# First mixture's results added to the residual inside the masked readout

## The chip, the cores and the metric

One core of one Trainium2 chip runs the whole program. The metric is device time in microseconds (us) of one execution. The kernel before took 2452.74 us, the median of 3 runs (2448.83 to 2454.53).

## The reference, cut to what matters

The reference is four layers, each an attention and a feed-forward part on x of 16 x 128 tokens x 256 numbers (B = 16 tiles of P = 128 rows, D = 256), float32. The change lies between the feed-forward part of layer 0 (a mixture of 8 experts, each token sent to 2) and the attention of layer 1 (a readout of a memory under a mask):

```python
x = x + _L0_ffn_ref(...)      # ends in: return hidden + moe_out, moe_out = the sum of two experts' weighted rows
x = x + _L1_xattn_ref(_layernorm(x), ctx_2048, mask)
x = x + _L1_ffn_ref(_layernorm(x), ...)           # ternary weights, inputs rounded to 8 bits

def _L1_xattn_ref(hidden_states, memory_tokens, memory_mask):
    scores = jnp.einsum('bsd,bmd->bsm', hidden_states, memory_tokens) * scale
    scores = jnp.where(memory_mask[:, None, :], scores, neg_inf)
    attn = jax.nn.softmax(scores, axis=-1)
    readout = jnp.einsum('bsm,bmd->bsd', attn, memory_tokens)
    return jnp.where(valid_b[:, None, None], readout, jnp.zeros_like(readout))
```

So the row that layer 1 starts from is (residual + hidden) + first expert's row + second expert's row.

## The kernel before, in words

The program is a chain of stages, each a block with a list of instructions for each of the five engines; an engine goes on to the next block when all engines have ended theirs. A stage works on pairs of tiles (PAIR = 2, so NI = 8 pairs, 128 x 512 numbers each). Waits are on semaphores, and the order of the work on each engine is written out by hand, the loops being unrolled.

`mixture0` (L1370) runs 39 blocks of 128 rows through the experts. TensorE first issues 18 matmuls of no use (`keep_busy`, L175), and then for each block turns the rows, multiplies and turns again. VectorE scales the results, and GpSimd scatters them by indirect DMAs into the DRAM tensor `expert_rows` (`taken`), the first expert's rows in its first half and the second's in its second half. Between the scatters GpSimd adds residual and hidden of each pair into `xk` (`residual_in`, L1498). When the last scatter has landed, `collect` (L1447) loads the two rows of each token back, four pairs in flight, VectorE's `combine` adds them (L1596 first expert's row plus `xk`, L1600 plus the second's), and SyncE stores each pair to `residual1`. The first pair is loaded again into `head` by `hand_on` (L162).

`mask_bit` (L3584) is the next stage. Its loop runs over steps i = 0 to 9; in a step the attention of pair i, the first feed-forward half of pair i-1 and the second of pair i-2 stand side by side. VectorE's list for a step is `softmax(i)`, `quantise2(i-2)` (it ends in the second rounding, two L3898), `product` (L3867), `readout(i)` (L3817 a reciprocal, L3820 a product of 128x2, L3824 the sum with x), `stats(i)`, `product`, `x_stats(i+1)` (L3791 to L3796), `product`, `quantise(i)` (L3843 to L3859), `x_norm(i+1)` (L3803), `product`, `residual(i-2)`, `subln(i-1)`. GpSimd's list is `rstd(i)` (L3698), `gain(i-1, 0)` (L3708), `x_rstd(i+1)` (L3694), `gain(i-1, 1)`, `rstd2(i-1)` (L3702). SyncE loads x (L3663) and the context (L3664, L3665) three pairs ahead into rings of XR = 3, waiting for `x2`, and stores the results. Stages that follow are not touched but for the counts of the two shared semaphores that are handed to them.

Of the kernel before, what the change touches and what calls it, by code (L numbers as in the profile page):

```python
# [1369 lines left out]
def mixture0(nc, k, x_in, src_in, out, spread, taken, arena, spare, bi, load_next, hand, ternary):  # L1370
# [7 lines left out]
    with ExitStack() as ctx:  # L1378
# [3 lines left out]
        def w(name):  # L1382
# [8 lines left out]
            gathered0 gathered1 gathered2 gathered3 first_added y stored0 stored1""")  # L1391
# [5 lines left out]
        xk = sb("xk", [P, B, D])  # L1397
# [7 lines left out]
        yg = spare[:, 0:16 * D].rearrange("p (r c t d) -> p r c t d", r=4, c=2, t=PAIR)  # L1405
        acc = spare[:, 16 * D:20 * D].rearrange("p (r t d) -> p r t d", r=2, t=PAIR)
        y = k["y"][:, hand["side"]].rearrange("p (r j d) -> p r j d", r=2, j=PAIR)
# [17 lines left out]
        @block.sync  # L1425
        def _(sp):
            def load_h(i):
                if i == NI - 1:
                    sp.wait_ge(k["last_stored"], hand["last"])
                if i >= 5:  # L1430
                    sp.wait_ge(s["res"], i - 3)
                sp.dma_start(h_pair(i), pair_of(src_in, i)).then_inc(s[f"h_loaded{i % 4}"], 16)

            def load_x(r, a, b):
                sp.dma_start(xk[:, a:b], x_in[a:b].rearrange("t p d -> p t d")).then_inc(s[f"x_loaded{r}"], 16)

            def load_rows(n, at):
                if n >= RR_:
                    sp.wait_ge(sent[f"kept_stored{n % YR}"], (n - RR_) // YR * 16 + 16)
                sp.dma_start(rows[:, n % RR_], spread[bass.ds(at, P)]).then_inc(s[f"rows_loaded{n % RR_}"], 16)  # L1440

            def collect(i):
                if i >= 4:
                    sp.wait_ge(s["y"], i - 3)
                for c in range(2):
                    first = (c * B + i * PAIR) * P
                    sp.dma_start(yg[:, i % 4, c], taken[first:first + PAIR * P].rearrange("(t p) d -> p t d", p=P)).then_inc(s[f"gathered{i % 4}"], 16)  # L1447

            def store(i):
                sp.wait_ge(s["y"], i + 1)  # L1450
                sp.dma_start(pair_of(out, i), y[:, i % 2]).then_inc(k["last_stored"] if i == NI - 1 else s[f"stored{i % 2}"], 16)

            sp.wait_ge(sent["scattered0"], 18 * 16)
            sp.wait_ge(sent["scattered1"], 14 * 16)
            for n in range(NB):
                load_rows(n, sp.value_load(bi[0:1, 1, n:n + 1], min_val=0, max_val=ROWS_SPREAD - P))
                if n == 3:
                    load_next[0](sp, s["weights_next"])
                if n == 8:
                    load_h(1)  # L1460
                    load_x(0, 2, 4)
                    load_h(2)
                    load_h(3)
                    load_x(1, 4, 8)
                    load_h(4)
                    load_x(2, 8, 16)
                if n in (16, 20, 24):
                    load_h(n // 4 + 1)
            for r in range(YR):
                sp.wait_ge(sent[f"kept_stored{r}"], (NB - r + YR - 1) // YR * 16)  # L1470
            for i in range(4):
                collect(i)
            for i in range(NI):
                store(i)
                if i + 4 < NI:
                    collect(i + 4)
                if i == 1:
                    sp.wait_ge(s["res"], 1)
                    sp.wait_ge(s["stored0"], 16)
                    hand_on(sp, k, hand)  # L1480
            for r in range(2):
                sp.wait_ge(s[f"stored{r}"], (NI // 2 - r) * 16)
            load_next[1](sp, s["weights_next"])
# [78 lines left out]
        def _(dve):  # L1562
# [30 lines left out]
            def combine(i):  # L1593
                dve.wait_ge(s[f"gathered{i % 4}"], (i // 4 + 1) * 32)
                dve.wait_ge(s["res"], i + 1)
                nc.vector.tensor_tensor(flat(acc[:, i % 2]), flat(yg[:, i % 4, 0]), flat(pair(xk, i)), ALU.add).then_inc(s["first_added"], 1)  # L1596
                dve.wait_ge(s["first_added"], i + 1)
                if i >= 2:
                    dve.wait_ge(s[f"stored{i % 2}"], i // 2 * 16)
                nc.vector.tensor_tensor(flat(y[:, i % 2]), flat(yg[:, i % 4, 1]), flat(acc[:, i % 2]), ALU.add).then_inc(s["y"], 1)  # L1600

# [11 lines left out]
            for i in range(NI):  # L1613
                combine(i)

        @block.tensor
        def _(pe):
# [34 lines left out]
            keep_busy(nc, k, 7, 18)  # L1652
# [1931 lines left out]
def mask_bit(nc, k, x_in, x_out, ctx_T, ctx_rows, masks, arena, load_next, hand, ternary):  # L3584
# [7 lines left out]
    with ExitStack() as ctx:  # L3592
# [3 lines left out]
        def w(name):  # L3596
# [4 lines left out]
            x_loaded0 x_loaded1 x_loaded2 t_loaded0 t_loaded1 t_loaded2 c_loaded0 c_loaded1 c_loaded2 stored0 stored1  # L3601
# [13 lines left out]
        xt = sb("xt", [P, XR, PAIR, D])  # L3615
# [25 lines left out]
        def x_pair(i):  # L3641
            return k["head"][:, 0] if i == 0 else xt[:, i % XR]

        def x_ready(eng, i):
            if i == 0:
                eng.wait_ge(k["first_loaded"], hand["first"])
            else:
                eng.wait_ge(s[f"x_loaded{i % XR}"], (i // XR + (i % XR > 0)) * 16)
# [6 lines left out]
        def _(sp):  # L3655
            def load(i):
                if i >= XR:
                    sp.wait_ge(s["x2"], i - XR + 1)
                pair = slice(i * PAIR, (i + 1) * PAIR)
                if i == NI - 1:  # L3660
                    sp.wait_ge(k["last_stored"], hand["last"])
                if i >= 1:
                    sp.dma_start(xt[:, i % XR], pair_of(x_in, i)).then_inc(s[f"x_loaded{i % XR}"], 16)  # L3663
# [25 lines left out]
        def _(pool):  # L3689
            nc.gpsimd.memset(ones[:], 1.0).then_inc(s["constants"], 1)  # L3690

            def x_rstd(i):
# [17 lines left out]
            x_rstd(0)  # L3710
            clear_spent(nc, k)
            for i in range(NI + 1):
# [4 lines left out]
                at(rstd2, i - 1)  # L3717

# [68 lines left out]
        def _(dve):  # L3787
            def x_stats(i):
# [119 lines left out]

            x_stats(0)
# [131 lines left out]
def build(nc, x, ctx_T, out, packs):  # L4041
# [8 lines left out]
    with ExitStack() as ctx:  # L4050
# [59 lines left out]
        with ExitStack() as kept:  # L4110
# [7 lines left out]
            mixture0(nc, k, res[0], hid, res[1], spread[0], taken[0], arena[0], arena[1][:, words(W_BIT):], bi, loader("bit", W_BIT, 1), hand(2, 4, 4, x1), ternary)  # L4118
            mask_bit(nc, k, res[1], res[0], ctx_T, x["ctx"], x["mask"], arena[1], loader("xatt2", W_XATT2, 0), hand(3, 5, 5, x0), ternary)
        xatt2(nc, k, res[0], res[1], ctx_T, arena[0], loader("arrow", W_ARROW, 1), hand(4, 6, 6, x1))  # L4120
        arrow(nc, k, res[1], res[0], arena[1], loader("qkv3", W_QKV3, 0), hand(5, 7, 8, x0))
        with ExitStack() as kept:
# [7 lines left out]
            qkv3(nc, k, res[0], ctx_T, qT, steps, KT, V, v_step, arena[0], nothing, hand(6, 8, 10), q_rows, q_ahead)  # L4130
            attend3(nc, k, qT, steps, att, KT, V, v_step, arena[0], loader("moe3", W_MOE3, 1), hand(7, 10, 12, x0, (1, att)), q_ahead)
        mixture3(nc, k, res[0], att, out, spread[1], taken[1], arena[1], arena[0], hand(8, 12, 14))
# [100 lines left out]
```

## Time and profile before

| what | value |
|---|---|
| median of 3 runs | 2452.74 us |
| the profiled execution, its own time | 2454.85 us |
| span of the profiled execution | 2453.1 us |
| mean granted TensorE clock | 0.944 of full speed |
| busy: TensorE, VectorE, ScalarE, GpSimd | 86%, 74%, 61%, 28% of the span |
| `expert_rows` loaded back | 32 DMAs of 256 KB in two stages, 4.6 us from issue to landing (median) |

The span runs from the first to the last instruction of one execution. Busy shares are averages over stages that have different limits; the rows of the next but one section are of the two stages in question.

### The profile page before, as it was taken

Reading aid. Unit: us, or ns where it says so; the run is one execution under the profiler, and the core shown is the slowest. Engines: PE = TensorE matmul, PEld = TensorE weight load, DVE = VectorE, ACT = ScalarE, POOL = GpSimd, SP = SyncE. Lnnn points to the kernel's source line nnn. Section 1 sums busy time; section 2 is a strip of 40 time slices with the busy share of each in tenths; the row PEclk is TensorE's granted clock in tenths of the full one; section 3 lists DMA queues with packets and bytes.
Section 4 is the critical chain, followed back from the end, with each engine's and each line's share of the span. In section 5 each row is a group of like instructions: output and inputs, shape, how many; then the busy total and the mean of one; then the engine's idle time right before and its main releaser. Section 6 shows DMA issues by size and latency. Waiting matters only on the chain. (4 is left out here: it accounts for less than half of the span.)

```text
span 2453.1 us, 49624 instructions
## 1 busy us (share of the span) xinstructions
PE 2111.5 (86%) x17715; PEld 1432.1 (58%) x17715; DVE 1805.0 (74%) x4336; ACT 1498.7 (61%) x2838; POOL 676.8 (28%) x820
## 2 busy tenths in 40 slices
PE   6987999999869748769979877899999999998897
PEld 4663666666646524447746665555555555556675
DVE  6866778788632358866647779899999999995434
ACT  4553666666524326634434445899999999993332
POOL 2214333535333413332213214211111111113532
PEclk9997999999979869989989999899999999999899
DMA  5543111211135251021010033466655655552234
GB/s 193 161 149 122 54 44 44 70 42 57 40 101 185 62 197 57 14 85 38 25 46 27 20 103 100 151 120 116 118 117 120 124 119 115 119 110 72 79 98 141
DMA packets 380704, 230.05 MB, mean 94 GB/s; under 512 B 270106, under 2 KB 372270, under 8 KB 379440
## 3 DMA queue, kind: packets, MB, share of 16 engines
q1 hardware_dynamic: 373648, 210.03, 32.2%
q0 software_dynamic: 6816, 16.86, 1.9%
q8 instruction: 146, 2.39, 0.4%
q14 instruction: 94, 0.77, 0.1%
HBM read 86.48 MB, written 77.68 MB: 67 GB/s over the span
## 5 line engine op out<-in xcount | busy, mean ns | idle before, releaser
L3488 DVE CUSTOM_DVE_ANT_0 arena<-psum,attend_zero,queries_step 128x1024 f32<-128x1024 f32 x512 | 622.4, 1279 | 13.6 <-PE psum L3537 13.2
L3462 ACT ACTIVATE attend_ex<-arena,attend_mx 128x2048 uint16<-128x2048 f32 x256 | 523.7, 2046 | 6.7 <-POOL attend_mx L3440 3.0
L3537 PE MATMUL psum<-keys_turned,queries_ahead 96*128 96x512 bf16 x1024 | 318.7, 394 | 41.7 <-DVE attend_mx L3488 25.4
L3562 PEld LDWEIGHTS psum<-values,attend_pw 128*128 128x128 f16 x4096 | 178.4, 97 | 124.5 <-issue 8.7
L3440 POOL TENSOR_SCALAR attend_mx<-attend_mx 128x1 f32<-128x1 f32 x256 | 73.9, 289 | 572.0 <-DVE attend_mx L3488 572.0
L3553 PE MATMUL psum<-keys_turned,ident_b 96*128 96x512 bf16 x510 | 195.1, 383 | 0.0
L3562 PE MATMUL psum<-values,attend_pw 128*128 128x16 f16 x4096 | 178.7, 170 | 0.2 <-DVE attend_pw L3509 0.2
L3467 ACT COPY attend_pw<-psum 128x512 f32<-128x512 f32 x263 | 161.4, 617 | 15.0 <-PE psum L3547 14.9
L3547 PE MATMUL psum<-ident_b,attend_ex 128*128 128x128 bf16 x2128 | 166.5, 222 | 3.6 <-ACT attend_pw L3467 1.4
L3547 PEld LDWEIGHTS psum<-ident_b,attend_ex 128*128 128x128 bf16 x2128 | 142.6, 99 | 40.9 <-ACT attend_ex L3462 6.6
L3537 PEld LDWEIGHTS psum<-keys_turned,queries_ahead 96*128 96x128 bf16 x1024 | 71.7, 99 | 120.6 <-DVE attend_mx L3488 109.1
L845 POOL TENSOR_TENSOR gqa_nq<-gqa_nq,neg_half 128x20 f32<-128x20 f32 x16 | 88.3, 5516 | 142.0 <-DVE gqa_nq L1042 142.0
L1255 PE MATMUL psum<-arena,gqa_hT 128*128 128x512 f32 x256 | 113.5, 596 | 0.0
L1343 PE MATMUL psum<-arena,gqa_pT 128*128 128x256 f32 x512 | 113.1, 379 | 0.0
L1343 PEld LDWEIGHTS psum<-arena,gqa_pT 128*128 128x128 f32 x512 | 97.3, 190 | 20.1 <-issue 7.7
L935 ACT ACTIVATE gqa_pr<-gqa_pr,gqa_mx 128x128 f32<-128x128 f32 x256 | 98.9, 390 | 6.5 <-DVE gqa_mx L1064 6.5
L848 POOL TENSOR_TENSOR gqa_ra<-gqa_ra,gqa_nq 128x2560 f32<-128x2560 f32 x16 | 71.5, 4467 | 49.6 <-DVE gqa_ra L1052 49.6
L1255 PEld LDWEIGHTS psum<-arena,gqa_hT 128*128 128x128 f32 x256 | 48.1, 192 | 55.6 <-issue 55.2
L177 PE MATMUL psum<-ident_b 128*128 128x512 bf16 x221 | 60.8, 420 | 10.7 <-PEq L707 8.5
L1064 DVE CUSTOM_DVE_ANT_0 gqa_pr<-psum,gqa_cmask 128x128 f32<-128x128 f32 x256 | 57.6, 287 | 16.6 <-PE psum L1276 12.7
L1276 PE MATMUL psum<-gqa_qkT 128*128 128x128 f32 x512 | 64.3, 280 | 0.0
L2851 POOL TENSOR_TENSOR arrow_outer<-arrow_vr,arrow_nr 128x1024 f32<-128x1024 f32 x16 | 30.9, 1932 | 117.2 <-DVE arrow_vr L2945 117.2
(578 smaller groups left out, 4920.9 us busy)
## 6 DMA issues: line engine op xcount, KB each, us to landing
spread_rows<-zeros SPq DMA_DIRECT2D x34, 1032.0 KB
moe_rows<-spread_rows SPq DMA_DIRECT2D x78, 129.0 KB, 2.1
arena<-expert_rows SPq DMA_DIRECT2D x32, 256.0 KB, 4.6
arena<-in_moe SPq DMA_DIRECT2D x1, 6344.0 KB, 19.8
residual<-stored_rows SPq DMA_DIRECT2D x48, 128.0 KB, 1.8
queries_turned<-queries_rows SPq DMA_DIRECT2D x16, 384.0 KB, 3.2
queries_ahead<-queries_turned SPq DMA_DIRECT2D x16, 384.0 KB, 4.0
arena<-in_gqa SPq DMA_DIRECT2D x1, 5440.0 KB, 17.9
```

Source lines behind the costliest of these rows:

```text
L845: nc.gpsimd.tensor_tensor(nq[:, j, 1], nq[:, j, 0], k["neg_half"][:].to_broadcast([P, HQK]), ALU.pow).then_inc(s["q_rms"], 1)
L935: last = nc.scalar.activation(pr[:, g], pr[:, g], ACT.Exp, bias=mx[:, 0, g:g + 1], scale=-1.0, accum_out=mx[:, 1, g:g + 1])
L1255: last = nc.tensor.matmul(BIG[:, b], hT[:, ic], wq[:, ic, b * 512:(b + 1) * 512], start=ic == 0, stop=ic == DC - 1)
L1343: last = nc.tensor.matmul(Y, oT[:, c], wo[:, c], start=c == 0, stop=c == GH - 1)
L3440: nc.gpsimd.tensor_scalar(mx[:, t % 2, h, 2:3], mx[:, t % 2, h, 0:1], mx[:, t % 2, h, 1:2], LN255, ALU.min, ALU.add).then_inc(s["bias"], 1)
L3462: nc.scalar.activation(ex[:, u % ER:u % ER + 2], kept[:, u % KR:u % KR + 2], ACT.Exp, bias=mx[:, t % 2, h, 2:3], scale=-1.0, accum_out=sum ...
L3467: nc.scalar.copy(pw[:, u % ER], TPW[:, turned_ahead[u] % TR]).then_inc(s["evacuated"], 1)
L3488: nc.vector.tensor_tensor_reduce(kept[:, u % KR], S[:, u % 2], zero[:].to_broadcast([P, UK]), steps[:, t, h:h + 1], 3.0e38, ALU.add, ALU.m ...
L3537: last = nc.tensor.matmul(S[:, u % 2, b * 512:(b + 1) * 512], qt[:, t % 2, h * P:(h + 1) * P], KT[:, c:c + 4, h // 2], start=True, stop=True)
L3547: last = nc.tensor.transpose(TP[:, rank % TR, c], counts[u % ER][:, c * P:(c + 1) * P], k["ident_b"][:])
L3553: nc.tensor.matmul(IDLE, k["ident_b"][0:W3], KT[:, c:c + 4, 0], start=True, stop=True)
L3562: last = nc.tensor.matmul(O[:, h * HD:(h + 1) * HD], pT[u % ER][:, c], V[:, kc, h * HD:(h + 1) * HD], start=kc == 0, stop=kc == B - 1)
```

## The change

`mixture0` no longer combines or stores. `xk` becomes a tensor `mixed_rows` that outlives the stage, SyncE loads only the first pair's expert rows ahead of its end, and the 18 matmuls at its start become 10. In `mask_bit` SyncE loads the expert rows of the other pairs into a ring of three, VectorE adds those of the first pair (`form_first`), and GpSimd those of the seven others (`form`): the first two as soon as they are there, each later one, of pair i, when VectorE has ended the second rounding of pair i-3. `residual1` is no longer written and read between the two stages.

```diff
...
+def collect_pair(sp, taken, results, i, done):
+
+
+    for c in range(2):
+        first = (c * B + i * PAIR) * P
+        rows = taken[first:first + PAIR * P].rearrange("(t p) d -> p t d", p=P)
+        sp.dma_start(results["y"][:, i % 3, c], rows).then_inc(done, 16)
+
+
+def mixture0(nc, k, x_in, src_in, spread, taken, arena, bi, load_next, hand, ternary, results):
...
-        xk = sb("xk", [P, B, D])
+        xk = results["x"]
...
-        yg = spare[:, 0:16 * D].rearrange("p (r c t d) -> p r c t d", r=4, c=2, t=PAIR)
-        acc = spare[:, 16 * D:20 * D].rearrange("p (r t d) -> p r t d", r=2, t=PAIR)
-        y = k["y"][:, hand["side"]].rearrange("p (r j d) -> p r j d", r=2, j=PAIR)
...
-            def collect(i):
-                if i >= 4:
-                    sp.wait_ge(s["y"], i - 3)
-                for c in range(2):
-                    first = (c * B + i * PAIR) * P
-                    sp.dma_start(yg[:, i % 4, c], taken[first:first + PAIR * P].rearrange("(t p) d -> p t d", p=P)).then_inc(s[f"gathered{i % 4}"], 16)
-
-            def store(i):
-                sp.wait_ge(s["y"], i + 1)
-                sp.dma_start(pair_of(out, i), y[:, i % 2]).then_inc(k["last_stored"] if i == NI - 1 else s[f"stored{i % 2}"], 16)
 
...
-            for i in range(4):
-                collect(i)
-            for i in range(NI):
-                store(i)
-                if i + 4 < NI:
-                    collect(i + 4)
-                if i == 1:
-                    sp.wait_ge(s["res"], 1)
-                    sp.wait_ge(s["stored0"], 16)
-                    hand_on(sp, k, hand)
-            for r in range(2):
-                sp.wait_ge(s[f"stored{r}"], (NI // 2 - r) * 16)
+            collect_pair(sp, taken, results, 0, k["first_loaded"])
             load_next[1](sp, s["weights_next"])
...
-            def combine(i):
-                dve.wait_ge(s[f"gathered{i % 4}"], (i // 4 + 1) * 32)
-                dve.wait_ge(s["res"], i + 1)
-                nc.vector.tensor_tensor(flat(acc[:, i % 2]), flat(yg[:, i % 4, 0]), flat(pair(xk, i)), ALU.add).then_inc(s["first_added"], 1)
-                dve.wait_ge(s["first_added"], i + 1)
-                if i >= 2:
-                    dve.wait_ge(s[f"stored{i % 2}"], i // 2 * 16)
-                nc.vector.tensor_tensor(flat(y[:, i % 2]), flat(yg[:, i % 4, 1]), flat(acc[:, i % 2]), ALU.add).then_inc(s["y"], 1)
-
...
-            for i in range(NI):
-                combine(i)
...
-            keep_busy(nc, k, 7, 18)
+            keep_busy(nc, k, 7, 10)
...
-def mask_bit(nc, k, x_in, x_out, ctx_T, ctx_rows, masks, arena, load_next, hand, ternary):
+def mask_bit(nc, k, taken, results, x_out, ctx_T, ctx_rows, masks, arena, load_next, hand, ternary):
...
-            x_loaded0 x_loaded1 x_loaded2 t_loaded0 t_loaded1 t_loaded2 c_loaded0 c_loaded1 c_loaded2 stored0 stored1
+            first_added pair_added first_formed pair_formed collected0 collected1 collected2 t_loaded0 t_loaded1 t_loaded2 c_loaded0 c_loaded1 c_loaded2 stored0 stored1
...
-        xt = sb("xt", [P, XR, PAIR, D])
+        yt = results["y"]
...
         def x_pair(i):
-            return k["head"][:, 0] if i == 0 else xt[:, i % XR]
+            return results["x"][:, i * PAIR:(i + 1) * PAIR]
 
         def x_ready(eng, i):
             if i == 0:
-                eng.wait_ge(k["first_loaded"], hand["first"])
+                eng.wait_ge(s["first_formed"], 1)
             else:
-                eng.wait_ge(s[f"x_loaded{i % XR}"], (i // XR + (i % XR > 0)) * 16)
+                eng.wait_ge(s["pair_formed"], i)
...
             def load(i):
+                pair = slice(i * PAIR, (i + 1) * PAIR)
+                if i >= XR:
+                    x_ready(sp, i - XR)
+                if i >= 1:
+                    collect_pair(sp, taken, results, i, s[f"collected{i % XR}"])
                 if i >= XR:
                     sp.wait_ge(s["x2"], i - XR + 1)
-                pair = slice(i * PAIR, (i + 1) * PAIR)
-                if i == NI - 1:
-                    sp.wait_ge(k["last_stored"], hand["last"])
-                if i >= 1:
-                    sp.dma_start(xt[:, i % XR], pair_of(x_in, i)).then_inc(s[f"x_loaded{i % XR}"], 16)
                 sp.dma_start(ct[:, i % XR], ctx_T[pair].rearrange("t p c m -> p t c m")).then_inc(s[f"t_loaded{i % XR}"], 16)
                 sp.dma_start(cr[:, i % XR], ctx_rows[pair].rearrange("t p d -> p t d")).then_inc(s[f"c_loaded{i % XR}"], 16)
 
...
+            def form(i):
+                x = flat(x_pair(i))
+                if i >= 3:
+                    pool.wait_ge(s["rounded2"], (i - 2) * PAIR)
+                pool.wait_ge(s[f"collected{i % XR}"], (i // XR + (i % XR > 0)) * 32)
+                nc.gpsimd.tensor_tensor(x, x, flat(yt[:, i % XR, 0]), ALU.add).then_inc(s["pair_added"], 1)
+                pool.wait_ge(s["pair_added"], i)
+                nc.gpsimd.tensor_tensor(x, x, flat(yt[:, i % XR, 1]), ALU.add).then_inc(s["pair_formed"], 1)
+
...
             x_rstd(0)
+            form(1)
             clear_spent(nc, k)
             for i in range(NI + 1):
                 at(rstd, i)
...
+                at(form, i + 2)
...
+            def form_first():
+                x = flat(x_pair(0))
+                dve.wait_ge(k["first_loaded"], hand["first"])
+                nc.vector.tensor_tensor(x, x, flat(yt[:, 0, 0]), ALU.add).then_inc(s["first_added"], 1)
+                dve.wait_ge(s["first_added"], 1)
+                nc.vector.tensor_tensor(x, x, flat(yt[:, 0, 1]), ALU.add).then_inc(s["first_formed"], 1)
+
...
+            form_first()
             x_stats(0)
             x_norm(0)
...
-            mixture0(nc, k, res[0], hid, res[1], spread[0], taken[0], arena[0], arena[1][:, words(W_BIT):], bi, loader("bit", W_BIT, 1), hand(2, 4, 4, x1), ternary)
-            mask_bit(nc, k, res[1], res[0], ctx_T, x["ctx"], x["mask"], arena[1], loader("xatt2", W_XATT2, 0), hand(3, 5, 5, x0), ternary)
-        xatt2(nc, k, res[0], res[1], ctx_T, arena[0], loader("arrow", W_ARROW, 1), hand(4, 6, 6, x1))
-        arrow(nc, k, res[1], res[0], arena[1], loader("qkv3", W_QKV3, 0), hand(5, 7, 8, x0))
+            results = dict(x=kept.enter_context(nc.sbuf_tensor("mixed_rows", [P, B, D], F32)),
+                           y=arena[1][:, words(W_BIT):words(W_BIT) + 12 * D].rearrange("p (r c t d) -> p r c t d", r=3, c=2, t=PAIR))
+            mixture0(nc, k, res[0], hid, spread[0], taken[0], arena[0], bi, loader("bit", W_BIT, 1), hand(2, 4, 4), ternary, results)
+            mask_bit(nc, k, taken[0], results, res[0], ctx_T, x["ctx"], x["mask"], arena[1], loader("xatt2", W_XATT2, 0), hand(3, 6, 4, x0), ternary)
+        xatt2(nc, k, res[0], res[1], ctx_T, arena[0], loader("arrow", W_ARROW, 1), hand(4, 7, 5, x1))
+        arrow(nc, k, res[1], res[0], arena[1], loader("qkv3", W_QKV3, 0), hand(5, 8, 7, x0))
...
-            qkv3(nc, k, res[0], ctx_T, qT, steps, KT, V, v_step, arena[0], nothing, hand(6, 8, 10), q_rows, q_ahead)
-            attend3(nc, k, qT, steps, att, KT, V, v_step, arena[0], loader("moe3", W_MOE3, 1), hand(7, 10, 12, x0, (1, att)), q_ahead)
-        mixture3(nc, k, res[0], att, out, spread[1], taken[1], arena[1], arena[0], hand(8, 12, 14))
+            qkv3(nc, k, res[0], ctx_T, qT, steps, KT, V, v_step, arena[0], nothing, hand(6, 9, 9), q_rows, q_ahead)
+            attend3(nc, k, qT, steps, att, KT, V, v_step, arena[0], loader("moe3", W_MOE3, 1), hand(7, 11, 11, x0, (1, att)), q_ahead)
+        mixture3(nc, k, res[0], att, out, spread[1], taken[1], arena[1], arena[0], hand(8, 13, 13))
         end_program(nc, k)
```

## Rows read from the trace of the kernel before

**Rows 1.** The page, part 1: busy us of each engine (share of the span) x instructions.

```profile
PE 2111.5 (86%) x17715; PEld 1432.1 (58%) x17715; DVE 1805.0 (74%) x4336; ACT 1498.7 (61%) x2838; POOL 676.8 (28%) x820
```

**Rows 2.** Busy time by stretch, around the change of stage: start:end, length, engines, clock, DMA.

```profile
860.00:870.00 10.00, 0.00 (x0) 0.00 (x0) 5.14 (x8) 0.00 (x0) 0.00 (x0) 0.50 1.02 321
870.00:880.00 10.00, 0.00 (x0) 0.00 (x0) 5.62 (x10) 0.00 (x0) 0.19 (x1) 0.50 0.81 280
880.00:890.00 10.00, 5.02 (x17) 3.68 (x18) 3.63 (x13) 2.68 (x6) 0.74 (x1) 0.50 0.84 275
```

**Rows 3.** The timeline where the stages meet: start, length, engine, line, operation [idle before].

```profile
857.31 3.97 SPq L1447 DMA_DIRECT2D arena<-expert_rows  x8
...
860.78 0.69 DVE L1596 TENSOR_TENSOR arena<-arena,moe_xk 128x512 f32<-128x512 f32 x1 [6.50 <-DMA arena<-expert_rows]
...
861.51 0.69 DVE L1600 TENSOR_TENSOR stored_rows<-arena 128x512 f32<-128x512 f32 x1
...
877.84 0.69 DVE L1600 TENSOR_TENSOR stored_rows<-arena 128x512 f32<-128x512 f32 x1
...
879.77 0.65 SPq L3672 DMA_DIRECT2D mbit_mi<-in_mask  x1
...
879.81 0.75 DVE L3791 BATCH_NORM_STATS2 mbit_st<-head 128x6 f32<-128x256 f32 x2 [1.28 <-PEq L1378]
```

**Rows 4.** The timeline of step 0 of the masked readout.

```profile
881.14 0.74 POOL L3694 TENSOR_TENSOR mbit_xs<-mbit_xs,neg_half 128x2 f32<-128x2 f32 x1 [1.17 <-DVE mbit_xs L3796]
...
881.91 0.73 DVE L3803 TENSOR_SCALAR mbit_xn<-head,mbit_mv,mbit_xs 128x256 f32<-128x256 f32 x2 [0.86 <-POOL mbit_xs L3694]
...
882.56 1.21 DVE L3912 TENSOR_SCALAR mbit_nm<-mbit_mi 1x2048 f32<-1x2048 int32 x1
...
884.54 1.19 PE L3977 MATMUL psum<-mbit_ct,mbit_xT 128*128 128x128 f32 x4 [0.72 <-ACT mbit_xT L3723]
...
896.67 0.78 POOL L3694 TENSOR_TENSOR mbit_xs<-mbit_xs,neg_half 128x2 f32<-128x2 f32 x1 [0.45 <-DVE mbit_xs L3796]
...
897.99 0.17 DVE L3848 TENSOR_SCALAR mbit_bs<-mbit_bs 128x2 f32<-128x2 f32 x1
...
898.39 0.62 DVE L3853 TENSOR_SCALAR mbit_bn<-mbit_bn,mbit_bs 128x256 f32<-128x256 f32 x2
```

**Rows 5.** The timeline of VectorE and GpSimd in step 2, last row of step 3.

```profile
925.09 1.42 DVE L3898 TENSOR_SCALAR mbit_ag<-mbit_ag,mbit_bs 128x1024 f32<-128x1024 f32 x2
...
927.21 0.16 DVE L3820 TENSOR_TENSOR mbit_xs<-mbit_xs 128x2 f32<-128x2 f32 x1
...
929.63 0.69 POOL L3698 TENSOR_TENSOR mbit_bs<-mbit_bs,neg_half 128x2 f32<-128x2 f32 x1 [5.57 <-DVE mbit_bs L3835]
...
930.10 0.74 DVE L3791 BATCH_NORM_STATS2 mbit_st<-mbit_xt 128x6 f32<-128x256 f32 x2
...
946.85 0.88 DVE L3824 SCALAR_TENSOR_TENSOR mbit_x<-psum,mbit_xs,mbit_xt 128x256 f32<-128x256 f32 x2 [1.11 <-PE psum L4016]
```

**Rows 6.** The timeline: a GpSimd sum, and the VectorE operation that began in it, twice.

```profile
911.93 2.36 POOL L3708 TENSOR_TENSOR mbit_ag<-mbit_a,arena 128x1024 f32<-128x1024 f32 x1
...
912.77 1.53 DVE L3796 TENSOR_SCALAR mbit_xs<-mbit_mv 128x2 f32<-128x2 f32 x1
...
469.80 4.47 POOL L848 TENSOR_TENSOR gqa_ra<-gqa_ra,gqa_nq 128x2560 f32<-128x2560 f32 x1 [3.08 <-DVE gqa_ra L1052]
...
472.89 1.39 DVE L1097 SCALAR_TENSOR_TENSOR gqa_sm<-gqa_mv 128x1 f32<-128x1 f32 x1
```

**Rows 7.** Two lines, all their instructions: ns min/median/max, first and last start.

```profile
L1498 POOL TENSOR_TENSOR moe_xk<-moe_xk,moe_ht x7: 1250/1291/1301, 773.3 to 830.3; 128x512 f32<-128x512 f32 x7
...
L3796 DVE TENSOR_SCALAR mbit_xs<-mbit_mv x8: 169/1510/1534, 880.9 to 1007.3; 128x2 f32<-128x2 f32 x8
```

**Rows 8.** TensorE in the timeline of the first mixture's start.

```profile
727.09 6.44 PE L177 MATMUL psum<-ident_b 128*128 128x512 bf16 x18 [8.51 <-PEq L707]
...
743.81 0.44 PE L1625 MATMUL psum<-ident,moe_rows 128*128 128x128 f32 x2 [3.10 <-DMA moe_rows<-spread_rows]
```

More of the change, by code:

```diff
@@ L1367, in _ @@
             rank(4)
-def mixture0(nc, k, x_in, src_in, out, spread, taken, arena, spare, bi, load_next, hand, ternary):
+def collect_pair(sp, taken, results, i, done):
[4 more added lines that the diff above has]
+def mixture0(nc, k, x_in, src_in, spread, taken, arena, bi, load_next, hand, ternary, results):
     NB = B * P * 2 // P + E - 1
@@ L1390, in mixture0 @@
             block_gu block_silu block_h hidden_turned hidden_copied block_y block_kept
-            gathered0 gathered1 gathered2 gathered3 first_added y stored0 stored1""")
+            """)
         sent = k["sent"][0]
```

## The prediction

> **What bounds the kernel now.** I read the page's busy shares first: TensorE 86% and VectorE 74% of 2453.1 us, GpSimd 28% [rows 1]. These are averages, and the change is local, so the second view is busy time by stretch. From 860 to 880 us TensorE, ScalarE and (but for a memset) GpSimd do nothing, VectorE is busy for half, and the DMA engines are all but full at 321 and 280 GB/s [rows 2]. That stretch is the combining of the first mixture, the third view. SyncE starts loading expert rows at 857.31, the first sum starts at 860.78, the last one at 877.84 with a length of 0.69, and the masked readout starts at 879.8 [rows 3]. Sixteen sums of 0.69 are 11 us of the 17.75 between first and last start plus length, and the rest is waiting for DMAs, so this stretch is bound by moving rows out and back in. No other engine has work in it, so all of it is on the path.
>
> In the masked readout the fourth view, the timeline of VectorE and GpSimd, shows VectorE as the pace: in step 2 its list goes on from one instruction to the next, and its waits are for GpSimd's sums and, in some steps, for TensorE (1.11 us in step 3 [rows 5]). GpSimd's list has free time from the end of `rstd2` to 929.63, where it had waited 5.57 us for VectorE [rows 5].
>
> **What goes: the combining.** Before, x_stats(0) starts at 879.81 [rows 3]. After, SyncE issues two loads from 857.31, at 3.97/8 = 0.50 each until 858.3. A stage begins 0.86 after SyncE's last issue in the old kernel (its last store, some 0.36 long, follows the last sum's end at 878.53, hence 878.9 to 879.77), so the next stage begins near 859.2. The first pair's rows are there at 860.78 as now, or a little sooner, since two loads are in flight and not eight; I leave it at 860.78. Two sums in a row end 1.42 later (861.51 + 0.69 = 862.20 [rows 3]), and x_stats(0) starts near 862.25. **The start of the readout moves by 17.6 us.** Ends: 15.6 if the change of stage takes 2 more, since it has had 20 us of idle engines to get its code in before; 18.1 if the rows land half a microsecond sooner.
>
> The removed stores, the reload of the first pair and the loads of x lie in the removed stretch or beside work, and free DMA time.
>
> **What is added at the entry of the readout.** SyncE now issues 11 loads where it had 9 up to the weights (four of expert rows for two of x, and the mask and context as before), in my count 1.5 MB ahead of and including the rows of pair 1. At the 300 GB/s of this stretch [rows 2] these are down near 864.5. The context of pair 0 is in front of them and starts 20.6 us earlier for a reader that moves by 17.6, so scores(0) doesn't wait for it.
>
> GpSimd's `form(1)` stands behind x_rstd(0), which ends at 881.88 - 17.6 = 864.3 [rows 4]. Its sums are of 128x512: 1.29 us each in the first mixture [rows 7], 2.6 to 2.7 for the two. Here the fifth view matters: what VectorE does under a GpSimd sum. A tensor_scalar of 128x2 that starts at 912.77 lasts 1.53 and ends at 914.30, just as the GpSimd sum does (911.93 + 2.36 = 914.29) [rows 6]; over its eight instructions the line goes from 169 ns to 1534, with a median of 1510 [rows 7]. So such an operation stands still until GpSimd's ends. x_norm(0) starts at 881.91 and the mask's conversion at 882.56, 1.21 long [rows 4], which are 864.3 and 865.0 after, just where `form(1)` can begin. If the rows land first, x_norm waits for up to two sums; if they land later, only the conversion does, which scores(0) need at 884.54 - 17.6 and which ends 0.77 ahead of them [rows 4]. Ends 0 and 2.6; I take the middle, **1.3 us**.
>
> GpSimd's `form(2)` stands behind x_rstd(1), which ends at 897.45 [rows 4] (old time base). Its rows have landed. It then runs to 900.1, and the 128x2 tensor_scalar at 897.99 and the rounding at 898.39 fall in it. The first is held until 898.8, the second until 900.1; its two instructions then end near 900.5 and not 899.01. TensorE and ScalarE stand waiting behind this rounding, so it is on the path: **1.5 us**, ends 0 and 2.6.
>
> **What is added in steps 2 to 6.** `form(3)` to `form(7)` each begin when the second rounding of a step ends. In step 2 that is 925.09 + 1.42 = 926.51 [rows 5]. Two sums: 926.6 to 927.9 and 928.0 to 929.3. The next GpSimd instruction starts at 929.63 and x_stats(3), which needs the pair, at 930.10 [rows 5], so neither waits, by 0.3 and 0.8 us. Of VectorE's list between 926.5 and 929.3 the operations on PSUM and the statistics have ordinary lengths elsewhere under GpSimd sums. The one left is L3820 at 927.21, a product with both inputs in SBUF [rows 5]. No row shows a tensor_tensor of that kind under a sum, but a scalar_tensor_tensor with both inputs in SBUF, 128x1, starts at 472.89 under one and ends at 474.28, with the sum's 474.27 [rows 6]. I take L3820 as held: it ends at 927.88 where it ended at 927.37, 0.5 us late.
>
> The Trainium skill, "SBUF — State Buffer", section "SBUF: two separate sides", says that VectorE operations with two SBUF inputs, or in a two-port mode, and a GpSimd operation take one shared port pair in turns, each for its whole length. By that rule L3820 is held, as taken here; were the rule only for two-port modes, the sum would be 1.5 us lower. The trace agrees for the scalar_tensor_tensor (1.39 us for 128x1) and has nothing on L3820.
>
> In step 3 readout(i) waits 1.11 us for TensorE behind L3820 [rows 5], and in step 5 the timeline has a like wait, so there the 0.5 is covered; without that cover it is paid. In steps 2, 4 and 6 it is paid: 3 x 0.5 = **1.5 us**. Ends: 0 (nothing held, or slack found) and 5 x 1.3 = 6.5 (each L3820 held for a whole sum). What the cover in step 3 was is TensorE's own lateness, so it can turn up in another step.
>
> **The 18 matmuls that become 10.** They take 6.44 us from 727.09, at first at the lower clock [rows 8]. Eight fewer let block 0 start up to 1.8 us sooner. But block 4 waits for its rows until 743.81, after 3.10 us of idle TensorE [rows 8]: those rows come behind the weights of the next stage (7168 words a row in the layout, 3.7 MB). So the start made sooner only lengthens that wait: **0**. Ends: -1.8 (were it to pass through) and +2 (TensorE idle for longer at 741 to 744 and its clock lower afterwards; after the idle stretch at 860 the clock is at half [rows 2], after this one it isn't yet).
>
> **The sum.** -17.6 + 1.3 + 1.5 + 1.5 + 0 = -13.3 us. The profiled execution took 2454.85 (span 2453.1 and 1.75 around it), so its like would be 2441.5. It stands 2.1 above the median of the runs, 2452.74; against that median I predict 2439.4.
>
> **Rivals.**
> - *The sums cost nothing* (chance 0.17). Rows of pair 1 land after the conversion, L3820 isn't held or its 0.5 us falls into slack, and TensorE, idle for 12 us and not 29, may be faster in step 0. For it: every held operation is short, and DMA is crowded at the entry. Against: 897.99 and 898.39 lie squarely in `form(2)`. Price: -17.6 to -18.1 with 1 for form(2): 2435.5.
> - *VectorE is held in every step, or the entry is late* (0.15). The sums slide by some tenths, so that the 128x2 tensor_scalar of stats(i) falls under the second one: held until its end, and with it five steps x 1.0 more; or the change of stage takes 2 longer. Price: -13.3 + 5 = -8.3: 2444.5. For it: the margin is 0.3 us. Against: the start of `form` hangs on VectorE's own rounding, so both move together.
> - *GpSimd's list becomes the loop* (0.03), the side on which it is slower. `form` stands ahead of rstd(i+1) and the gains; rounding, sums, x_stats, x_norm, scores and the next rounding would be one ring. GpSimd then sets the pace only if its sums, begun at 926.6, end more than 0.8 later than 929.3; beyond this point each microsecond of delay counts in each of five steps. To eat 13.3 takes 2.7 more a step, sums of 2.7 us each and not 1.29. Price at 4 us a step: +20 - 13.3: 2459.5. Against: seven sums of this size lie between 1250 and 1301 ns [rows 7].
> - *The stretch isn't saved* (0.02): the DMA time comes back, since the same 4 MB of expert rows are still read. Against: the loads of later pairs wait for a free slot, not for bandwidth, and the stores are gone. Price: within 3 us of before.
>
> My forecast has the remaining 0.63. A shift of all later stages can move TensorE's clock by a few us either way; that widens the range, not the middle. Range for 8 in 10: 2432 to 2447. A change under 0.2% (4.9 us) can't be told from none here. Faster by more: 0.95; within: 0.03; slower: 0.02.
>
> **What would show it.** The next stage's first instruction at 859 to 861 and the first x_stats at 862.2; GpSimd sums of 1.29 us, two at a time, right behind each pair of L3898; L3820 at some 0.67 us and not 0.16 in steps 2 to 6; L3848 and one L3853 of step 0 longer than 0.6; the readout's end 13 us earlier; TensorE's wait at 743.8 still there and longer by a microsecond. It is wrong if the first x_stats comes after 865, if waits for the new sums stand ahead of x_stats(i), or if later stages differ by over 3 us.

## The result, and the profile after

The changed kernel took 2436.22 us, the median of 5 runs (2434.39 to 2437.88), and the kernel before, now also with 5 runs, 2449.49 (2446.29 to 2454.53). The ratio is 0.9940, 95% interval 0.9924 to 0.9955. That is 13.3 us by the medians; the forecast was 13.3 us, and 2439.4. Two more comparisons of the same pair gave 0.9939 (0.9926 to 0.9952) and 0.9947 (0.9932 to 0.9962), 15.1 and 14.7 us by the medians.

The two profiled executions differ by more, 18.6 us of span. First the page of the kernel after, for [rows 1], and then its timeline where the stages meet, for [rows 3]:

```profile
span 2434.5 us, 49580 instructions
...
PE 2104.8 (86%) x17707; PEld 1431.4 (59%) x17707; DVE 1799.1 (74%) x4322; ACT 1498.1 (62%) x2838; POOL 693.5 (28%) x834
```

```profile
850.90 0.97 POOL L1490 DMA_INDIRECT expert_rows<-moe_yk,moe_rows  x1 [0.93 <-DVE moe_yk L1575]
...
853.14 0.90 SPq L1376 DMA_DIRECT2D arena<-expert_rows  x2
855.36 0.65 SPq L3645 DMA_DIRECT2D mbit_mi<-in_mask  x1
...
856.62 0.69 DVE L3775 TENSOR_TENSOR mixed_rows<-mixed_rows,arena 128x512 f32<-128x512 f32 x1 [6.50 <-DMA arena<-expert_rows]
...
857.35 0.69 DVE L3777 TENSOR_TENSOR mixed_rows<-mixed_rows,arena 128x512 f32<-128x512 f32 x1
858.08 0.75 DVE L3782 BATCH_NORM_STATS2 mbit_st<-mixed_rows 128x6 f32<-128x256 f32 x2
...
860.83 1.21 DVE L3904 TENSOR_SCALAR mbit_nm<-mbit_mi 1x2048 f32<-1x2048 int32 x1
...
862.09 1.26 POOL L3670 TENSOR_TENSOR mixed_rows<-mixed_rows,arena 128x512 f32<-128x512 f32 x1 [1.95 <-DMA arena<-expert_rows]
```

The next stage begins 2.2 us after SyncE's first load, under cover of the 3.48 us that the rows take to land, and the first statistics come right behind two sums. To place the rest, I took the same marks in both timelines (us):

| from, to | before | after | difference |
|---|---|---|---|
| start, first matmul of the mixture | 727.09 | 725.27 | -1.82 |
| to the start of the last scatter | 127.97 | 125.63 | -2.34 |
| to x_stats(0) | 24.75 | 7.18 | -17.57 |
| to x_stats(1) | 15.55 | 15.54 | -0.01 |
| to softmax(1) | 9.50 | 11.81 | +2.31 |
| to the second rounding of step 2 | 20.23 | 20.24 | +0.01 |
| to the end of the readout's stage | 135.22 | 135.27 | +0.05 |
| to the end of the span | 1392.79 | 1393.56 | +0.77 |

The lines from the last scatter to the end of the readout are the change's own, and in these two traces they add up to -15.2. The first line is of stages that it doesn't touch. So is the last. The second was in dispute, since the 10 matmuls stand there.

One pair of traces isn't the whole answer. The same stretch, from the last scatter to the end of the readout, took 205.26 us here and 203.96 in the other trace with the old readout (before_keep10, below), and 189.97 to 190.53 in the four traces with the changed one and no edit in this stretch (after, after_again, keep18, after_c). So the change is worth 13.4 to 15.3 us there, and the medians (13.3, 15.1 and 14.7) lie in or at this band. The line to softmax(1) moves most: it is 8.44 in before_keep10 and not 9.50, and 11.39 to 12.01 in the four. The experiment late2 comes back to it.

Step 0 of the readout after, for the last rows of [rows 4], VectorE and GpSimd:

```profile
875.68 1.26 POOL L3670 TENSOR_TENSOR mixed_rows<-mixed_rows,arena 128x512 f32<-128x512 f32 x1
876.25 0.72 DVE L3839 TENSOR_SCALAR mbit_bs<-mbit_bs 128x2 f32<-128x2 f32 x1
...
877.02 1.26 POOL L3672 TENSOR_TENSOR mixed_rows<-mixed_rows,arena 128x512 f32<-128x512 f32 x1
877.20 1.49 DVE L3844 TENSOR_SCALAR mbit_bn<-mbit_bn,mbit_bs 128x256 f32<-128x256 f32 x2
...
885.43 0.42 DVE L3800 TENSOR_REDUCE mbit_xs<-psum 128x2 f32<-128x256 f32 x1 [5.56 <-PE psum L3970]
```

The small tensor_scalar went from 0.17 to 0.72 and the rounding from 0.62 to 1.49; each ends within a few hundredths of the sum above it, or one operation behind. And step 2, for [rows 5], from VectorE's and GpSimd's timelines:

```profile
905.67 1.42 DVE L3889 TENSOR_SCALAR mbit_ag<-mbit_ag,mbit_bs 128x1024 f32<-128x1024 f32 x2
...
907.80 0.67 DVE L3811 TENSOR_TENSOR mbit_xs<-mbit_xs 128x2 f32<-128x2 f32 x1
...
911.20 0.74 DVE L3782 BATCH_NORM_STATS2 mbit_st<-mixed_rows 128x6 f32<-128x256 f32 x2
```

```profile
907.17 1.27 POOL L3670 TENSOR_TENSOR mixed_rows<-mixed_rows,arena 128x512 f32<-128x512 f32 x1 [2.52 <-DVE mbit_ag L3889]
908.51 1.27 POOL L3672 TENSOR_TENSOR mixed_rows<-mixed_rows,arena 128x512 f32<-128x512 f32 x1
910.73 0.70 POOL L3680 TENSOR_TENSOR mbit_bs<-mbit_bs,neg_half 128x2 f32<-128x2 f32 x1 [0.95 <-DVE mbit_bs L3826]
```

The sums start 0.08 after the rounding, L3811 is held until the first of them ends (907.17 + 1.27 = 908.44, and 907.80 + 0.67 = 908.47), and GpSimd is free again 0.95 before its next work. L3811 lasts 0.67 in steps 2 to 6 and 0.16 in the others.

The waits for TensorE in steps 3 and 5 of the kernel before are gone. Where they come from shows in the granted clock. This is step 3 of the kernel before, around the wait that ends at 946.85 [rows 5] (columns: start:end, length, then busy us and instructions of PE, PEld, DVE, ACT and POOL, the granted clock as a share of full, the DMA share and GB/s):

```profile
942.00:944.00 2.00, 0.92 (x5) 0.51 (x6) 1.63 (x9) 1.74 (x6) 0.43 (x1) 0.90 0.01 4
944.00:946.00 2.00, 2.00 (x6) 1.41 (x5) 1.70 (x5) 1.98 (x4) 0.00 (x0) 0.50 0.00 0
946.00:948.00 2.00, 2.00 (x14) 1.24 (x14) 1.12 (x3) 1.99 (x3) 0.00 (x0) 0.75 0.00 0
```

TensorE ran at half its clock from 943.6 to 947.0. In all thirteen traces of this document the readout waits 0.6 us or more for TensorE in steps 2 to 7 eleven times (1.31 at most, in nine traces), and each time the wait lies in such a stretch of 3.4 us or ends within 0.4 us of its end. The traces without such a wait have no low stretch in steps 3 to 7 (after, after_c, nowait, and vsum, which has one in step 2 and a wait of only 0.32).

### The profile page after: what moved, and what is told of

It reads as the page before. It is cut to its first block and busy times, and to the rows that moved or that the text cites. A ratio compares the mean times of both kernels' runs of the same rounds, so it can differ in the third digit from the quotient of the medians.

```text
span 2434.5 us, 49580 instructions
## 1 busy us (share of the span) xinstructions
PE 2104.8 (86%) x17707; PEld 1431.4 (59%) x17707; DVE 1799.1 (74%) x4322; ACT 1498.1 (62%) x2838; POOL 693.5 (28%) x834
## 5 line engine op out<-in xcount | busy, mean ns | idle before, releaser
L3440 ACT COPY attend_pw<-psum 128x512 f32<-128x512 f32 x263 | 158.7, 608 | 15.1 <-PE psum L3520 15.0
L845 POOL TENSOR_TENSOR gqa_nq<-gqa_nq,neg_half 128x20 f32<-128x20 f32 x16 | 88.2, 5515 | 140.5 <-DVE gqa_nq L1042 140.5
```

What stands on the lines that cost most here:

```text
L845: nc.gpsimd.tensor_tensor(nq[:, j, 1], nq[:, j, 0], k["neg_half"][:].to_broadcast([P, HQK]), ALU.pow).then_inc(s["q_rms"], 1)
L3440: nc.scalar.copy(pw[:, u % ER], TPW[:, turned_ahead[u] % TR]).then_inc(s["evacuated"], 1)
```

## The experiments

Theory: the gain is the 17.6 us at the change of stage; it is paid for where VectorE's operations with two SBUF inputs, or tensor_scalars from SBUF to SBUF, lie under a GpSimd sum. Rivals: the matmuls of no use have a part in it; the place of the sums doesn't matter. The first four of the table ran on one chip, the next four on a second, the last three on a third; on the second the changed kernel itself wasn't run, so there the traces and the ratios have to do.

| kernel | median us | before, same chip | ratio (95%) |
|---|---|---|---|
| after_again | 2434.96 | 2450.03 | 0.9939 (0.9926 to 0.9952) |
| keep18 | 2434.04 | 2450.03 | 0.9936 (0.9923 to 0.9949) |
| before_keep10 | 2449.33 | 2450.03 | 0.9992 (0.9982 to 1.0003) |
| nowait | 2443.38 | 2450.03 | 0.9970 (0.9960 to 0.9981) |
| late2 | 2422.79 | 2441.58 | 0.9926 (0.9913 to 0.9939) |
| split | 2423.25 | 2441.58 | 0.9927 (0.9914 to 0.9939) |
| both | 2422.48 | 2441.58 | 0.9923 (0.9905 to 0.9940) |
| vsum | 2435.45 | 2441.58 | 0.9975 (0.9964 to 0.9986) |
| after_c | 2436.22 | 2450.88 | 0.9947 (0.9932 to 0.9962) |
| late2_c | 2433.14 | 2450.88 | 0.9933 (0.9918 to 0.9947) |
| both_c | 2431.25 | 2450.88 | 0.9921 (0.9906 to 0.9936) |

**The same kernel again.** No edit.

> The changed kernel once more, beside the three below on one chip. Theory: some 13 to 15 us (0.54% to 0.61%) under the kernel before, since by the two traces 17.6 us go at the change of stage, 2.3 are given back in step 0 of the readout, and the rest of the difference of the traces (18.6 us) lies in stages that change from run to run. Rival (the whole 18.6 us belong to the change): 0.76% under before. In the trace both expect first x_stats 7.2 us after the last scatter's start, and L3811 at 0.67 us in steps 2 to 6.

15.1 us under before. In its trace the last scatter and x_stats(0) are 7.14 apart (7.18 in the first), and L3811 is 0.66 to 0.67 five times. That lies a hair above the theory's 13 to 15 and well under the rival's 18.6: the whole 18.6 us were not the change's.

**The matmuls of no use.**

```diff
-            keep_busy(nc, k, 7, 10)      # the changed kernel -> keep18
+            keep_busy(nc, k, 7, 18)
-            keep_busy(nc, k, 7, 18)      # the kernel before -> before_keep10
+            keep_busy(nc, k, 7, 10)
```

> The changed kernel with 18 matmuls at the start of the first mixture, as before. My theory from the prediction: those matmuls have no part in it, since block 4 waits for its rows in either case; the time is that of the changed kernel within 1 us, and the mixture from its first matmul to its last scatter may differ by the clock only. Rival: the 10 gave the 2.3 us by which the mixture was shorter after (125.6 and not 128.0 us from first matmul to last scatter); then this kernel is 2.3 us slower than the changed one and its mixture takes 128.0 us.

> The kernel before with the one edit of 10 matmuls for 18. If they have no part: the time of before within 1 us. If they give 2.3 us: 2.3 us (0.09%) faster, the mixture 125.6 us from first matmul to last scatter and TensorE's idle stretch before block 4 about 5.0 us and not 3.1.

Neither edit moved the time clear of its interval: 0.9 us faster with 18 than with 10, and 0.7 us faster with 10 in the kernel before. TensorE in the timeline of the mixture's start, after and in keep18, for [rows 8]:

```profile
725.27 4.42 PE L177 MATMUL psum<-ident_b 128*128 128x512 bf16 x10 [8.33 <-PEq L707]
...
742.11 0.69 PE L1598 MATMUL psum<-ident,moe_rows 128*128 128x128 f32 x2 [5.01 <-DMA moe_rows<-spread_rows]
```

```profile
726.16 6.80 PE L177 MATMUL psum<-ident_b 128*128 128x512 bf16 x18 [8.29 <-PEq L707]
```

Block 4 starts 16.84 us after the first matmul (16.72 before), so the 2.0 us saved in front turned into wait, 5.01 and not 3.10 (5.20 in before_keep10, 2.99 in keep18). From first matmul to last scatter the two traces with 18 have 127.97 (before) and 126.51 (keep18); of the eleven with 10, ten have 125.3 to 126.1 (125.63 in after) and nowait has 128.38. So the mixture may be some 0.4 to 2.7 us shorter with 10, and two traces with 18 can't settle it. The medians show no such gain (keep18 is the faster one), but their intervals are some 3 us to either side. What is shown is the trade of start for wait; that the edit has no part at all isn't, and the 2.3 us of the table above are not shown to be of it either.

**No wait for the rounding** (nowait).

```diff
-                if i >= 3:
-                    pool.wait_ge(s["rounded2"], (i - 2) * PAIR)
```

> The changed kernel without GpSimd's wait for the second rounding: form(3) to form(7) then start right after rstd2. Theory (port held for a whole GpSimd sum): the two sums, 2.6 us, lie over the small VectorE operations with two SBUF inputs and over the rounding itself; the rounding ends about 1.5 to 2.5 us later than after in each of steps 2 to 6, in all 6 to 12 us slower than the changed kernel. Rival (the place of the sums doesn't matter, since VectorE loses a like time wherever they stand): within 2 us of the changed kernel.

8.4 us slower than after_again. The timelines of GpSimd and VectorE in step 2:

```profile
907.74 1.27 POOL L3668 TENSOR_TENSOR mixed_rows<-mixed_rows,arena 128x512 f32<-128x512 f32 x1
909.09 1.27 POOL L3670 TENSOR_TENSOR mixed_rows<-mixed_rows,arena 128x512 f32<-128x512 f32 x1
```

```profile
907.82 1.22 DVE L3874 TENSOR_TENSOR mbit_bs<-mbit_bs 128x2 f32<-128x2 f32 x1 [0.20 <-POOL mbit_bs L3682]
...
909.26 1.12 DVE L3879 TENSOR_SCALAR mbit_bs<-mbit_bs 128x2 f32<-128x2 f32 x1
...
910.82 1.42 DVE L3887 TENSOR_SCALAR mbit_ag<-mbit_ag,mbit_bs 128x1024 f32<-128x1024 f32 x2
```

Each sum holds one operation of 0.16, for 1.22 and 1.12, so the rounding is 22.26 after softmax(1) and not 20.24, the next four steps take 20.39 and not 18.90, and the one after them 18.40, since it has no sums over it. The place of the sums is worth 2.0 us once, 1.5 four times and -0.5 once, 7.5 in all. The rival falls.

**The second pair's sums later** (late2).

```diff
+                if i == 2:
+                    pool.wait_ge(s["x_normed"], 2)
```

> The changed kernel with the sums of pair 2 waiting for x_norm(1) (VectorE's L3794 of step 0). Theory: in the changed kernel these sums hold L3839 and L3844 in step 0, 1.4 us on the path; moved behind x_norm(1) they lie in VectorE's wait for the scores, so softmax(1) comes 1.4 to 2.3 us sooner after x_stats(1) (11.8 to 12.0 us now, 9.5 before) and the kernel is 1.4 to 2.3 us faster. Rival (the 2.3 us of step 0 are TensorE's clock): the step stays within 0.5 us of 11.8.

Against before on its chip 18.8 us, with nothing else beside it to say how much of that is the edit. The trace says where it acts, VectorE and GpSimd in step 0:

```profile
872.72 0.61 DVE L3846 TENSOR_SCALAR mbit_bn<-mbit_bn,mbit_bs 128x256 f32<-128x256 f32 x2
...
874.58 1.28 POOL L3672 TENSOR_TENSOR mixed_rows<-mixed_rows,arena 128x512 f32<-128x512 f32 x1 [2.79 <-DVE mbit_xn L3796]
...
878.13 0.42 DVE L3802 TENSOR_REDUCE mbit_xs<-psum 128x2 f32<-128x256 f32 x1 [3.63 <-PE psum L3972]
```

The rounding is back at 0.61, and x_stats(1) to softmax(1) takes 8.44, 3.4 less than in the kernel after. 1.4 of this are the sums. The rest shows in the granted clock of this stretch, after and in late2:

```profile
877.00:879.00 2.00, 0.00 (x0) 0.00 (x0) 1.89 (x6) 0.27 (x1) 1.26 (x1) 0.62 0.10 34
879.00:881.00 2.00, 1.50 (x9) 1.35 (x10) 0.86 (x3) 1.04 (x2) 0.00 (x0) 0.50 0.00 0
881.00:883.00 2.00, 2.00 (x8) 1.10 (x6) 0.00 (x0) 0.58 (x1) 0.00 (x0) 0.50 0.00 0
```

```profile
873.00:875.00 2.00, 0.84 (x8) 0.67 (x9) 1.43 (x7) 1.14 (x2) 0.42 (x1) 1.00 0.17 58
875.00:877.00 2.00, 2.00 (x13) 1.19 (x11) 0.00 (x0) 0.75 (x2) 1.92 (x2) 1.00 0.00 0
```

In the kernel after, TensorE was idle for 4.1 us, waiting for the late rounding, and its clock went to the lower level (0.5 of 2.4 GHz) for the scores; in late2 it was idle for 2.8 and stayed at the upper. But the length of the idle stretch doesn't decide it. The kernel before, without any sum there, was idle for only 2.69, and has the low clock too:

```profile
899.82 0.61 PE L3952 MATMUL psum<-ident_b,mbit_bq 128*128 128x128 bf16 x4 [2.69 <-ACT mbit_bq L3760]
```

```profile
899.00:901.00 2.00, 1.18 (x8) 1.12 (x9) 1.10 (x6) 1.26 (x2) 0.00 (x0) 0.55 0.00 0
901.00:903.00 2.00, 2.00 (x9) 1.08 (x8) 0.00 (x0) 0.63 (x2) 0.00 (x0) 0.59 0.00 0
```

By all traces, with this rounding not held, x_stats(1) to softmax(1) takes 8.43 to 8.44 without a low stretch (before_keep10, late2, late2_c) and 9.49 to 9.53 with one of 3.4 us (before, both, both_c); vsum, below, has 10.38 with one of 6.8. With it held there was a low stretch every time, of 3.4 to 10.2 us, and the time was 11.38 to 12.60 (after, after_again, keep18, split, after_c, nowait). So the sums cost 1.4 by the hold, and with the clock 1.9 to 4.2 in all. Late2's gain of 3.4 is the 1.4 and a clock that stayed up; why it stays up in one trace and not in another isn't shown.

**The product as two operations** (split), and **both edits** (both).

```diff
-                nc.vector.tensor_tensor(r[:, 7], r[:, 6], r[:, 5], ALU.mult).then_inc(s["factor"], 1)
+                for j in range(PAIR):
+                    last = nc.vector.tensor_scalar(r[:, 7, j:j + 1], r[:, 6, j:j + 1], r[:, 5, j:j + 1], None, ALU.mult)
+                last.then_inc(s["factor"], 1)
```

> The changed kernel with the product L3811 (two SBUF inputs, 128x2) made as two tensor_scalars of 128x1 with a pointer scalar. Theory: those are not held by GpSimd's sum, the readout starts 0.4 us sooner in steps 2 to 6 and a step takes 18.5 us and not 18.9, so up to 2 us faster. Rival: what VectorE gains it waits for TensorE (1.1 to 1.3 us in steps 3 and 5 of the kernel before), steps come to 18.4 and 19.4 in turn and the kernel is within 1 us of the changed one.

> The changed kernel with both edits (the wait of the second pair's sums for x_norm(1), and L3811 as two tensor_scalars). Theory: the two gains add, 1.4 to 2.3 and 0 to 2 us: 1.5 to 4 us faster than the changed kernel. Rival: the shifts only move TensorE's waits and the clock's low stretches, within 1 us of it.

GpSimd and VectorE of split in step 2:

```profile
900.37 1.27 POOL L3670 TENSOR_TENSOR mixed_rows<-mixed_rows,arena 128x512 f32<-128x512 f32 x1 [2.52 <-DVE mbit_ag L3891]
```

```profile
901.00 0.34 DVE L3812 TENSOR_SCALAR mbit_xs<-mbit_xs 128x1 f32<-128x1 f32 x2
901.37 0.88 DVE L3817 SCALAR_TENSOR_TENSOR mbit_x<-psum,mbit_xs,mixed_rows 128x256 f32<-128x256 f32 x2
```

Under the same sum the two take 0.34 and are not held. Three of five steps are 18.55 us and not 18.9, one is 18.79. The fifth was 19.64, with a wait of 1.13 for TensorE, so the second rounding of step 2 to the end is 135.13, where the kernel after has 135.27. In both it is 134.95, with a step of 19.82 and a wait of 1.08. Both theories had a part: the steps are shorter, and against the kernel after, which has no such wait, the one wait takes nearly all of it.

**The sums on VectorE** (vsum): `form` word for word on VectorE, ahead of x_stats of its pair, without the wait for the rounding; none on GpSimd.

> The changed kernel with the sums of pairs 1 to 7 on VectorE, right ahead of x_stats of the pair, none on GpSimd. Theory: VectorE is the pace of the readout, two sums cost it 1.42 us a step and nothing is held: steps of 18.4 + 1.4 = 19.8 us in place of 18.9, seven of them, so 4 to 7 us slower than the changed kernel. Rival (TensorE's waits in steps 3 and 5 take it up): 19.8 in some steps, 19.9 in those with the wait, 2 to 4 us slower.

2435.45 and 0.9975, outside the interval of every kernel with the sums on GpSimd but nowait. Against the changed kernel's ratio of 0.9940 that is some 8.5 us slower, more than theory or rival had. Steps took 20.6 to 20.8, 1.7 to 1.9 more than 18.9, where 1.42 in place of the 0.5 hold would give 0.9. One of GpSimd's gains and VectorE's second sum:

```profile
909.34 2.72 POOL L3681 TENSOR_TENSOR mbit_ag<-mbit_a,arena 128x1024 f32<-128x1024 f32 x1
```

```profile
909.87 2.73 DVE L3766 TENSOR_TENSOR mixed_rows<-mixed_rows,arena 128x512 f32<-128x512 f32 x1
```

The sum of 0.69 is held under the gain, which ends at 912.06, and ends at 912.60. The gain itself began under VectorE's first sum and took 2.72 where it takes 2.36 [rows 6]. My expectation that nothing is held was wrong: VectorE's sums have two SBUF inputs themselves, and the second one waits for GpSimd's product.

**Side by side.** The changed kernel, late2 and both once more on one chip.

> The changed kernel beside the two below, all on one chip, to set their times against it; 0.55% to 0.65% under the kernel before.

> The changed kernel with the sums of pair 2 behind x_norm(1), beside the changed one. In the trace step 0 was 3.4 us shorter than in the changed kernel (8.4 and 11.8 us from x_stats(1) to softmax(1)): 1.4 of sums no longer over VectorE's work, the rest TensorE at full clock in that step. Theory (both last): 2 to 3.4 us faster than the changed kernel. Rival (the clock's low stretch comes elsewhere): 0 to 1.4 us faster.

> Both edits, beside the changed kernel. If the steps of 18.55 us (in place of 18.9) count in full: 1 to 2 us faster than with the one edit. If TensorE's waits take it back (a step of 19.8 in its first trace): the same as with the one edit within 1 us.

2436.22, 2433.14 and 2431.25: 3.1 and 5.0 us under the changed kernel. Softmax(1) comes 11.78, 8.43 and 9.49 after x_stats(1). The intervals of late2_c and after_c overlap, those of both_c and after_c too, if by little (0.9936 and 0.9932); in the earlier comparison late2, split and both lay within 0.8 us of each other. The traces say more than the medians, for the stretch from the last scatter to the end of the readout: 189.97 to 190.53 in the four of the changed kernel and keep18, 189.33 in split, 187.14 and 186.73 in late2 and late2_c, 187.29 and 187.40 in both and both_c. So the later sums take some 3 us off the readout, and the second edit adds nothing to them that shows: with both edits the clock fell in step 0 and again in step 3, each time. The kernel with both edits has the lowest ratios of all (0.9921, 0.9923); that the whole program is faster than with the later sums alone is not shown.

## Why the prediction was right

- **The change of stage, -17.6.** Measured -17.57 in the trace; 7.14 and 7.19 us from last scatter to x_stats(0) in the other two traces of the same kernel. This term carries the prediction, and its mechanism is as worked out.
- **The first sums of GpSimd, +1.3.** Measured 0: the rows landed near 862.0, as late as the end of the mask's conversion (862.04). The case of my lower end. The term was mis-sized because the landing was: 3.9 us behind the start of x_stats(0), where I had the rows down 2.25 behind it (864.5 and 862.25). Here GpSimd began at 862.09 and had nothing of VectorE's to hold.
- **The second pair's sums, +1.5.** The rounding ended 1.42 later after x_stats(1), by the two holds named. What the term left out is TensorE's clock in that step, which depends on the trace: another 0.9 against before (+2.31 in all), another 2.0 against before_keep10 (+3.37 in all). The edit of late2 took the hold away; the low clock was gone as well in its two traces, but not in the two of the kernel with both edits.
- **Steps 2 to 6, +1.5.** The hold of L3811 until the sum's end, 0.5 each, is as worked out. Split shows that it goes when the product is made otherwise, but it changed the number of inputs and the size at once, so that it is the two inputs isn't shown apart from the size. Its price came out at +0.05, since the waits for TensorE in steps 3 and 5 of the kernel before, 1.1 and 1.3, were gone. I counted them as cover for the 0.5 and held them for fixed. They move with the low stretches of the clock: 0.80 in step 5 of after_again, 1.14 in step 7 of keep18, 1.26 and 0.70 in steps 3 and 6 of before_keep10. This step of the prediction was wrong in its reasoning: five holds were paid, 2.5 us, and two clock waits of 2.4 us in all happened not to come.
- **10 matmuls, 0.** Not contradicted by two experiments, which leave room for some 3 us to either side; TensorE's wait before block 4 grew by 1.9 where I had said one.
- **The sum.** -13.3 forecast; -15.2 by the marks (-13.4 to -15.3 over all traces), -13.3, -15.1 and -14.7 by the medians of three comparisons. That the first comparison agrees to the decimal is luck: of the three small terms one was 0 for 1.3, one 2.3 for 1.5 and one 0.05 for 1.5. The large one was right, and it decides the result.
- **Rivals.** "The sums cost nothing" is right that the rows of pair 1 land after the conversion, and the holds of L3820 cost nothing in this pair of traces; it is wrong that TensorE is faster in step 0 (15.54 and 15.55 us from x_stats(0) to x_stats(1)) and wrong on form(2). GpSimd's list never set the pace: it had 0.93 to 0.95 us left in each of steps 2 to 6. The later stages differed by 0.8 us; the same code took from 1389.3 to 1393.6 us in the first six traces, so my sign of 3 us could not have told much.

## What to carry to other kernels

A stretch in which only DMAs and one engine work, between two stages, is the cheapest to remove: move its first piece to the next stage's start and its rest under that stage, and the gain can be read off two timeline rows. Before putting work on GpSimd, list VectorE's instructions in that span by inputs: those with two SBUF inputs, and tensor_scalars of more than one element from SBUF, wait for the end of the GpSimd sum or product, and a 0.16 us operation can cost 1.2. A wait for another engine that comes and goes with TensorE's clock is not a fixed cover; price the edit with and without it, and read a difference of a microsecond or two only out of several traces of each kernel.

## What the runs showed of the hardware that was not expected

VectorE operations of 128x1 with a pointer scalar, all in SBUF, were not held under a GpSimd sum (0.34 for two), where the 128x2 product with two inputs took 0.67. A hold of 1.4 us on VectorE cost 3.4 us at the step's end from after to late2, the rest being TensorE's lower clock; yet the clock also fell in step 0 of before and both, behind idle stretches of 2.69 and 2.66 us, and not in before_keep10, behind 3.27. And a VectorE sum that began during a GpSimd product lasted 2.73 us in place of 0.69. Not every GpSimd operation holds VectorE: in an earlier stage of the kernel before (gqa), 128x1024 products of two SBUF inputs begin under a GpSimd power of 128x20 that lasts 5.5 us (L845) and take their 1.24 us sixteen times out of sixteen.
